# Decoder layer on one core: batch 0's cross-attention scores computed in three f32r passes, its context split into high and low parts by ScalarE and GpSimd

## What is computed

```
x = x + self_attention(layernorm(x)) @ Wo          # 32 heads of 16, 8 key heads
Q = layernorm(x) @ Wq.T + bq ; K = ctx @ Wk.T + bk
scores = Q @ K.T / sqrt(512) ; x = x + softmax(scores) @ ctx
q = round(clip(w / (mean|w| + 1e-5), -1, 1))        # for gate, up, down
x = x + ((h @ gate.T) * (h @ up.T)) @ down.T        # h = layernorm(x)
```

## Time and profile before

| | |
|---|---|
| median of 3 runs | 226.55 us (226.46 to 226.76) |
| the profiled execution | 226.59 us, its span 224.8 us |
| granted TensorE clock | 1.00 of full speed over the whole span |
| PE busy | 209.1 us (93%), 1492 instructions |
| DVE busy | 147.7 us (66%) |
| ACT busy | 124.9 us (56%) |
| POOL busy | 65.8 us (29%) |
| chain that ended last | PE 76%, DVE 7%, ACT 6%, issue 5%, DMA 3% |

### The profile page before, as it was taken

One profiled execution on the slowest core, in us unless ns is written; L12 is line 12 of the kernel. 1 busy time (PEld: TensorE's weight loads), 2 busy tenths in 40 slices (PEclk: granted clock), 3 DMA queues, 4 the chain that ended last, 5 costly groups with the idle time before them and its releaser, 6 DMA issues.

```text
span 224.8 us, 4335 instructions
## 1 busy us (share of the span) xinstructions
PE 209.1 (93%) x1492; PEld 151.8 (68%) x1500; DVE 147.7 (66%) x556; ACT 124.9 (56%) x210; POOL 65.8 (29%) x87
## 2 busy tenths in 40 slices
...
GB/s 168 371 397 417 209 0 1 3 52 204 223 80 51 93 52 0 188 122 309 31 4 0 199 176 0 3 0 3 0 0 1 3 0 3 0 93 0 3 0 95
DMA packets 9078, 19.98 MB, mean 89 GB/s; under 512 B 1152, under 2 KB 1536, under 8 KB 9056
## 3 DMA queue, kind: packets, MB, share of 16 engines
...
q10 hardware_dynamic: 576, 0.10, 0.2%
...
## 4 chain that ended last, share of the span: by engine, by line
PE 76%; DVE 7%; ACT 6%; issue 5%; DMA 3%; SPq 1%; DVEq 0%; POOL 0%; ACTq 0%
PE ps L1376 17%; PE ps L1230 13%; PE ps L1391 8%; PE ps L1267 5%; PE ps L1298 3%; PE ps L1329 3%; PE ps L1210 3%; DMA wqkv<-wqkv_dram 3%; PE ps L1439 3%; PE ps L1164 3%; PE ps L1521 3%; PE ps L1450 2%; PE ps L1480 2%; PE ps L1179 2%; PE ps L1189 2%
## 5 line engine op out<-in xcount | busy, mean ns | idle before, releaser
L1048 DVE CUSTOM_DVE_ANT_0 ps<-ps,maskf 128x128 f32<-128x128 f32 (+1 forms) x128 | 41.1, 394 | 3.1 <-PE ps L1450 2.1
L584 POOL TENSOR_SCALAR_AFFINE_SELECT prob<-prob 128x512 f32<-128x512 f32 x32 | 19.8, 643 | 49.0 <-ACT prob L802 48.9
L802 ACT ACTIVATE prob<-ps 128x1536 f32<-128x1536 f32 x16 | 23.3, 1454 | 19.3 <-PE ps L1486 19.3
L503 POOL TENSOR_TENSOR rstd<-veps,neghalf 128x1 f32<-128x1 f32 x12 | 7.3, 609 | 58.3 <-DVE veps L837 58.3
L672 ACT CAST in_hi<-inter 128x256 f16<-128x256 f32 (+1 forms) x22 | 8.9, 405 | 23.1 <-DVE inter L1001 23.1
L1376 PE MATMUL ps<-h_hi,gate_q 128*128 128x256 f16 (+1 forms) x88 | 20.5, 273 | 0.0
L1376 PE MATMUL ps<-h_lo,up_q 128*128 128x256 f16 (+1 forms) x88 | 20.4, 273 | 0.0
L1376 PE MATMUL ps<-h_hi,up_q 128*128 128x256 f16 (+1 forms) x88 | 20.4, 273 | 0.0
L1376 PE MATMUL ps<-h_lo,gate_q 128*128 128x256 f16 (+1 forms) x88 | 20.4, 272 | 0.0
L1001 DVE TENSOR_TENSOR inter<-gate_s,ps 128x256 f32<-128x256 f32 (+1 forms) x22 | 9.2, 418 | 15.6 <-PE ps L1376 14.7
L665 ACT ACTIVATE gate_s<-ps 128x256 f32<-128x256 f32 (+1 forms) x22 | 8.4, 384 | 18.8 <-PE ps L1376 18.8
...
## 6 DMA issues: line engine op xcount, KB each, us to landing
...
```

The costliest lines, as they stand in the source:

```text
L584: nc.gpsimd.affine_select(out=v, in_=v, compare_op=ALU.is_ge, fill=0.0, base=0, pattern=[[0, GROUP], [1, P]], channel_multiplier=-1).then_ ...
L802: nc.scalar.activation(prob[:, i % 2, :], ps[:, 3:6, :].rearrange("p a b -> p (a b)"), ACT.Exp, scale=DH ** -0.5).then_inc(exp_done, 1)
L1048: nc.vector.tensor_tensor_reduce(scores, scores, mask, 1.0, LOWEST, ALU.add, ALU.max, to).then_inc(max_done, 1)
```

## The change

Batch 0's two score tiles (`xs` of tiles 0 and 1) go from four plain f32 matmuls to `three_passes`. For that ctx.T of batch 0 (`ctxT0`, four chunks of 128 x 512) is split: the high parts by four casts on ScalarE, the low parts by four subtractions on GpSimd (`low` of `ctxT0`, semaphore `ctx_low`). g of batch 0 is now evacuated like that of batch 1: high part on ScalarE into `gT0_r`, low part on VectorE into `gT0_lo`. The high parts of the context and `gT0_lo` lie where the projection weights `wqkv` lay. The ternary `down` weights lie there too, so their first chunk now waits until `xs` of tile 1 is computed and until the splits are done, and the absolute sums of `down` write their unused result elsewhere (`magnitudes`, over `roped`). One chunk of `whole` for `down` moves from VectorE to GpSimd, (2,1), and one the other way, (2,4). One `st` copy moves from ScalarE to VectorE. The table of pieces, the list behind the loop, the loads' places and the step of the `dot` column are new.

```diff
-        wqkv = sb("wqkv", [P, KD, QKV])
+        front = ExitStack()
+        wqkv = sb("wqkv", [P, KD, QKV], F32, front)
+        front.close()
+        ctxT0_hi = sb("ctxT0_hi", [P, KD, CTX], F32R)
+        gT0_lo = sb("gT0_lo", [P, KD, T], F32R)
...
-        POOL_CHUNKS = [(0, 0), (0, 1), (0, 2), (0, 3), (1, 0), (1, 1), (1, 2), (1, 3), (2, 4)]
+        POOL_CHUNKS = [(0, 0), (0, 1), (0, 2), (0, 3), (1, 0), (1, 1), (1, 2), (1, 3), (2, 1)]
...
-            ([("out", 10), ("max", 13)], [("a", 3, 1), ("n2", 1), ("tern", 1, 3)], [("xT", 1, 0), ("xT", 1, 1),
-             ("high", "wo", 0)]),
+            ([("n2", 0), ("out", 10), ("max", 13), ("tern", 1, 3)], [("a", 3, 1), ("n2", 1), ("high", "ctxT0", 3)],
+             [("xT", 1, 0), ("low", "ctxT0", 2), ("xT", 1, 1), ("abs", 2, 0)]),
...
-        COLUMN_AT = {17: ("sum", 2), 11: ("sum", 1), 3: ("sum", 0), 13: ("dot",)}
+        COLUMN_AT = {17: ("sum", 2), 11: ("sum", 1), 3: ("sum", 0), 12: ("dot",)}
...
-        ST_ON_ACT = (10, 11, 12, 14, 15, 17, 18)
+        ST_ON_ACT = (10, 11, 14, 15, 17, 18)
...
-        UP_LOADS, CTX_LOAD, DOWN_LOADS = {3: (0, 1), 4: (2,), 5: (3,)}, 6, {10: (0,), 12: (1,), 13: (2, 3)}
+        UP_LOADS, CTX_LOAD, DOWN_LOADS = {3: (0,), 4: (1, 2), 6: (3,)}, 5, {10: (0,), 12: (1, 2), 13: (3,)}
...
+                    if piece[0] == "low" and piece[1:] in POOL_SPLITS:
+                        name, k = piece[1:]
+                        pool.wait_ge(split_hi, SPLITS.index(piece[1:]) + 1)
+                        nc.gpsimd.tensor_tensor(low_part(name)[:, k, :], split[name][0][:, k, :],
+                                                split[name][1][:, k, :].bitcast(F32), ALU.subtract).then_inc(ctx_low, 1)
...
+                if w == 2 and c == 0:
+                    wait_side(act, "xs", 1)
+                    act.wait_ge(ctx_low, KD)
                 nc.scalar.activation(tern_target(w)[0:rows, at:at + n], raw[0:rows, at:at + n], ACT.Sign,
...
-                        if b == 1:
-                            wait_split(pe, "ctxT")
-                            mm = three_passes(to, lambda k: gT1_hi[:, k, cols], lambda k: gT1_lo[:, k, cols],
-                                              lambda k: ctxT1_hi[:, k, :], lambda k: low_part("ctxT")[:, k, :])
-                        for m in range(KD if b == 0 else 0):
-                            mm = nc.tensor.matmul(to, gT0[:, m, cols], ctxT[b][:, m, :],
-                                                  start=(m == 0), stop=(m == KD - 1))
+                        name, g_hi, g_lo = (("ctxT0", gT0_r, gT0_lo), ("ctxT", gT1_hi, gT1_lo))[b]
+                        wait_split(pe, name)
+                        mm = three_passes(to, lambda k: g_hi[:, k, cols], lambda k: g_lo[:, k, cols],
+                                          lambda k: split[name][1][:, k, :], lambda k: low_part(name)[:, k, :])
```

More of the change, by code:

```diff
@@ L144, in decoder_layer @@
         tail.close()
-        ctxT[0] = sb("ctxT0", [P, KD, CTX], F32, late)
+        ctxT[0], ctxT0_r = sb_twice("ctxT0", [P, KD, CTX], late)
         ctx_n[0] = sb("ctx_n0", [P, PT, D], F32, late)
@@ L303, in decoder_layer @@
-            ([("out", 10), ("max", 13)], [("a", 3, 1), ("n2", 1), ("tern", 1, 3)], [("xT", 1, 0), ("xT", 1, 1),
-             ("high", "wo", 0)]),
-            ([("out", 11), ("max", 14), ("abs", 2, 0), ("abs", 2, 1)], [("g", 0, 0), ("g", 0, 1)], [("abs", 2, 2),
-             ("low", "wo", 0), ("abs", 2, 3)]),
-            ([("max", 15), ("out", 12), ("xs", 0), ("low", "wo", 1), ("low", "wo", 2), ("high", "wo", 1)],
-             [("high", "wo", 2), ("part", 2), ("abs", 2, 4)], [("xs", 1), ("xpT", 0)]),
@@ new lines, in decoder_layer @@
+            ([("out", 5), ("u", 0), ("max", 8)], [], [("u", 1)]),
+            ([("out", 6), ("whole", 1, 0), ("max", 9)], [("part", 1)], [("whole", 1, 1), ("whole", 1, 2)]),
+            ([("out", 7), ("c",), ("max", 10)], [("whole", 1, 3), ("cc", 0)], [("low", "ctxT0", 0),
+             ("high", "ctxT0", 0), ("a", 2, 1)]),
+            ([("out", 8), ("tern", 1, 0), ("max", 11)], [("cc", 1), ("tern", 1, 1)], [("wo", 0), ("low", "ctxT0", 1)]),
+            ([("high", "ctxT0", 1), ("out", 9), ("max", 12), ("wo", 1)], [("tern", 1, 2), ("a", 3, 0)],
+             [("high", "ctxT0", 2)]),
@@ new lines, in decoder_layer @@
+            ([("n2", 0), ("out", 10), ("max", 13), ("tern", 1, 3)], [("a", 3, 1), ("n2", 1), ("high", "ctxT0", 3)],
+             [("xT", 1, 0), ("low", "ctxT0", 2), ("xT", 1, 1), ("abs", 2, 0)]),
+            ([("high", "wo", 0), ("max", 14), ("low", "ctxT0", 3), ("out", 11)], [("g", 0, 0), ("low", "wo", 0),
+             ("abs", 2, 1), ("g", 0, 1)], [("abs", 2, 2), ("high", "wo", 1), ("abs", 2, 3), ("low", "wo", 1)]),
+            ([("out", 12), ("max", 15), ("xs", 0), ("low", "wo", 2), ("high", "wo", 2), ("abs", 2, 4)], [],
+             [("part", 2), ("xs", 1), ("xpT", 0)]),
```

90 lines of the change are left out of this document (47 added, 43 removed).

## The result

The changed kernel takes **227.62 us** (median of 14 runs, 227.00 to 229.38), the kernel before 226.63 us (14 runs, 226.20 to 227.21): a ratio of 1.0056, 95% interval 1.0041 to 1.0071. It is 1.0 us slower, where 226.8 us and no change that can be told had been forecast.

A forecast was written before the change was run, and what follows sets the result against it. TensorE was taken to bound behind the loop, and TensorE, VectorE and ScalarE in turn inside it. New waits of +2.05 us, -1.40 in the tiles and -0.37 in step 19 gave +0.28 us: 226.8 us, range 225.6 to 227.7.

The forecast's parts named there:

- The two `xs` tiles: Batch 0's score tiles on TensorE: three f32r passes save 0.70 us a tile, -1.40 us for two.
- xn in step 19: VectorE's xn no longer runs beside a GpSimd chunk and goes from 0.92 back to 0.55 us: -0.37 us.
- The delays up to step 15's scores: New waits in steps 12 to 15: 0.5, 0.5, 0.4 and 0.25 us, and 0.2 us for GpSimd.
- step 12's +0.5: Step 12: `cc` 1 behind the scores adds 0.6 us, the moved dot column gives back about 0.1: +0.5 us.
- The cast in step 13: ScalarE in step 13: a cast of `ctxT0` between exponential and ternary chunk delays the output's turn by +0.5 us.
- `n2` 0: VectorE, steps 13 and 14: moved behind the row maxima, it makes the maxima's copy 1.9 us late, +0.4 us for TensorE.
- 0.25 behind it: Step 15's scores wait for VectorE's low part of `xT` 10, 1.65 us late against TensorE's own 1.4: +0.25 us.
- GpSimd beside VectorE: Steps 13 and 14: GpSimd's zeroing and subtraction slow the xn of `n2` 0 and `n2` 1: +0.2 us.
- The new wait at `xs` 0: Step 16: `xs` 0 now waits for both the high and the low part of `g` 0,1: +0.2 us.
- A: Rival: `n2` 0 costs nothing and GpSimd doesn't hold VectorE up; 226.0 us, or 225.5 if step 13's cast is covered; chance 0.28.
- B: Rival: an earlier absolute sum makes ScalarE wait for the loads of `down`; landing at 110.0 gives 227.8 us; chance 0.15.
- C: Rival: GpSimd holds VectorE fully during the xn of `n2` 0 and `n2` 1; 227.2 us; chance 0.10.

The follow-up runs named there:

- e3_plain_xs: Changed kernel with batch 0's two score tiles as four plain f32 matmuls each on the high parts, splits still made: 228.67 us, ratio 1.0095.
- e8_cc_only: Changed kernel with only `cc` 1 back ahead of step 12's scores: 227.95 us, ratio 1.0074.
- e7_cast_only: Changed kernel with only ScalarE's cast of `ctxT0` 1 moved from step 13 to step 12, behind `oT`: 226.77 us, ratio 1.0008.
- e1_n2_back: Changed kernel with only `n2` 0 back ahead of `wo` 1 in step 13, as in the kernel before: 226.88 us, ratio 1.0022.
- e9_low_later: e5_n2_cast with GpSimd's low part of `ctxT0` 1 moved from step 12 to step 13: 226.58 us, ratio 1.0003.
- e4_before_n2_late: Kernel before with only `n2` 0 moved to the head of step 14, as the change has it: 229.17 us, ratio 1.0096.
- e5_n2_cast: Changed kernel with `n2` 0 back ahead of `wo` 1 and ScalarE's cast of `ctxT0` 1 moved to step 12: 227.77 us, ratio 1.0067.

## Why the prediction was wrong

**The step that failed** is the sentence that the clock is granted in full over the whole span, so that durations are taken as they stand. It was read from the kernel before and carried over to a kernel whose waits the prediction itself made longer. It had computed a turn of `oT` 0.5 us later and a copy of mT for which TensorE would wait, one behind the other, and didn't ask what they do to the clock. In 6 of 14 runs it costs some 1.3 us. None of the rivals had it.

**The undisturbed sum** failed beside it: 0.28 forecast, 0.68 measured, and at the median this 0.40 us is more than the clock's 0.31. Two gains were taken too large, by 0.14 and 0.23 us; the delays came right in sum, 2.08 for 2.05, by two terms that missed in opposite directions.

- *The two `xs` tiles*, -1.40: the mechanism is right, the size is 0.60 + 0.66 = 1.26 us. The rows count from the end of the work before, which a tile's first matmul overlaps by different amounts: 0.16 us in the tile of 3.45, but 0.25 us in the `wo` tile of 2.75, whose first matmul starts ahead of 142.99:

```profile
142.74 0.48 PE L1230 MATMUL ps<-xwq_r,ctx_cols_hi 128*128 128x512 f32 x1
```

From its own first matmul to its last result that `wo` tile takes 3.00 us, the `xs` tiles 3.61 and 3.70 before and 3.01 and 3.05 after. e3_plain_xs, which puts plain matmuls in the same place, confirms the size: 228.62 - 227.31 = 1.3 us, and its tiles take 3.60 and 3.54 us from start to next start, 1.32 us more than the three passes.
- *xn in step 19*, -0.37: it is back at 0.55 us, as forecast, and the turned tile `xT` 2,1 does come 0.37 us earlier behind VectorE's addition (135.16 to 138.41, before 133.46 to 137.08). But 0.23 us is lost again ahead of the `wo` tile, where TensorE now idles 0.30 us: VectorE's subtraction ctx_cols_lo starts at 138.98, right behind the end of ScalarE's cast (138.36 + 0.59), and ends at 139.67. So 0.14 is left (from the work behind `xs` 1 to the `wo` tile, 15.38 us for 15.52).
- *The delays up to step 15's scores*, 0.5 + 0.5 + 0.4 + 0.25 and 0.2 for GpSimd, 1.85: measured 107.84 - 80.62 - 1.40 - 24.18 = 1.64. Each term was on a chain that runs beside others, so undoing one gives less or more than its entry. Of step 12's +0.5 the shift is 0.36, and `cc` 1 alone accounts for none of it (e8_cc_only), since the ternary chunks stood behind it. The cast in step 13, +0.5, gives 0.68 back, 0.5 of it in the stretch (e7_cast_only). `n2` 0, +0.4 and a share of the 0.25 behind it, gives 0.64 back, of which the stretch shows only 0.3, for the wait for xn opens in step 15 instead (e1_n2_back). Both together give only 0.74 (e9_low_later). Moved into the kernel before, `n2` 0 costs 1.4 us alone, in the stretch as in the time (e4_before_n2_late): there nearly all of its 1.65 us chain shows.
- *GpSimd beside VectorE*, +0.2 of these: xn of `n2` 0 takes 0.84 us instead of 0.55, that of `n2` 1 0.54. So +0.3 on VectorE's chain; what of it reaches TensorE isn't separated from the 1.64.
- *The new wait at `xs` 0*, +0.2: 0.44. From the start of g's second high part to `xs` 0 are 1.96 us (114.94 to 116.90), before 1.52 (112.42 to 113.94; the 114.10 of the prediction is the end of `oT`'s turn). The low part on VectorE ends at 116.69 and the turn of the maxima on TensorE at 116.73; the profile doesn't say which of the two `xs` 0 waited for.

Of the signs that the prediction named, the wait ahead of step 12's scores is 0.55 us (0.7 expected), the turn of output 10 comes 0.85 us later against the step's begin (1.0), the copy of maxima 13 is at 100.43 (100.7) with TensorE waiting for it, and TensorE has no gap behind the loop.

**The rivals.** A (the gain stays) is out: undisturbed runs are 0.68 us slower, and `n2` 0, which it had for nothing, costs 0.64 us here and 1.4 us in the kernel before. B (the loads of `down`) didn't happen; the absolute sum starts without a wait for a transfer, and the last load was issued at 103.14 instead of 104.07:

```profile
107.43 1.27 ACT L665 ACTIVATE roped<-raw 128x1280 bf16<-128x1280 f32 x1
108.61 0.19 ACT L665 ACTIVATION_READ_ACCUMULATOR roped<-raw 128x1 f32 x1
108.93 1.45 ACT L825 ACTIVATE prob<-ps 128x1536 f32<-128x1536 f32 x1
```

C (GpSimd holds VectorE for the whole overlap) is out for the size. xn of `n2` 0 overlaps GpSimd's zeroing, which ends at 97.82 + 1.23 = 99.05, by 0.57 us, and is 0.29 longer; that of e5_n2_cast overlaps by 1.20 us and is 0.93 longer. The Trainium skill (SBUF — State Buffer, "Who interferes with whom") has the second to issue blocked until the first ends, of a VectorE instruction in a two-port mode and a GpSimd one. That would be 0.57 and 1.20 us; these traces show half and three quarters of it. As a warning the rule was worth more than I gave it: e5_n2_cast loses 1 us by it.

**What stays open.** Why the clock falls in some executions of a kernel and not in others, and in those that were not profiled, at which of the two places it fell. e7_cast_only still has a wait of 0.49 and one of 0.86 us, as far apart as in the changed kernel, and fell in 2 of 12 runs, which took only 0.5 us more than its undisturbed ones. How much wait a stretch can hold without a fall isn't measured.
